# Expert weights and attention weights of the first half: the transfers start after ten gathers in place of two

## The chip, the core and the metric

One program on one core of a Trainium2 chip. The metric is the device time of one execution in microseconds (us). The five engines are called PE (matrix products), DVE (vector), ACT (scalar, activations), POOL (general) and SP (here it only issues transfers). Transfers issued by SP run on one hardware queue (q1), those issued by POOL on a software queue (q0); both are served by the core's 16 DMA engines.

## The reference

A block with three parts over x, 4 x 1024 tokens of width 256, all float32:

```python
x = x + 0.5 * ffn(layernorm(x), ...)      # mixture of 8 experts, first half
x = x + attn(layernorm(x), ...)           # gated recurrence, projections, MLP
x = x + 0.5 * ffn(layernorm(x), ...)      # the same 8 experts, second half

def ffn(tokens):                          # 4096 tokens
    probs = softmax(tokens @ gate_w + gate_b)
    expert_idx = argmax(probs)            # one expert for each token
    # the first 160 tokens of each expert are kept: 8 x 160 = 1280 slots
    h = gelu(dispatch @ w1[e] + b1[e])    # 256 -> 1024
    expert_out = h @ w2[e] + b2[e]        # 1024 -> 256
    # back to the token's row, times its probability; other rows get 0
```

The expert weights w1 and w2 have 1 MB each for each expert; the attention uses Wa (256 x 512), Wk, Wv, Wg, Wq, Wo (256 x 256), W1 (256 x 1024) and W2 (1024 x 256).

## The kernel before, in words

The program has three stages: the first expert half (about 0 to 142 us of the span), the attention (to about 620 us) and the second expert half. Only the first half is touched. Synchronisation is written by hand with semaphores: an engine's instructions run in the order of the code, and a wait holds back all that stands behind it on that engine.

**The first half on the computing engines.** x is read in 8 blocks (tiles `xc`), the gate's logits are computed, and a list of tokens for the 1280 slots is made. POOL then gathers the slots' rows from x in HBM with 10 indirect transfers of 128 rows each (L574, tile `xg`, semaphores `xg_in[0]` to `xg_in[9]`). DVE normalises a gathered tile (L240), PE turns it (L969, `turn_in`), ACT copies it to `xdt` (L811). An expert e is `up(e)` on PE (L982: 8 groups of products into four banks, each group followed by a GELU on ACT, L819) and `down(e)` (L995, then ACT L828). PE's order is turn_in 0 and 1, up(0), `list_gates` (L911), turn_in 2 to 4, up(1), turn_in 5 to 9, down(0), up(2), down(1), a turn_out (L1009), up(3), down(2), a turn_out, up(4), down(3) and so on to down(7). up(0) needs the gathers 0 and 1 alone, up(1) those up to 4 by the code's order. down(0) also waits for DVE's `idx_s` (L768), which stands behind all ten gathers' norms.

**The weights.** The experts' weights live in a ring of four buffers (`ring`, `GE = 4`): those of experts 0, 1 and 2 are fetched early, at 20 to 40 us; expert 3's (the "fourth expert's") goes to the fourth buffer, and those of 4 to 7 each to a buffer that a finished `down` sets free. `up(e)` waits for both transfers of expert e.

**The attention's raw weights.** DVE splits each weight matrix of the attention into a high and a low part (`w_in_h`, `w_in_l`, `w_h`, `w_l`; L776 and L778). There are ten pieces in this order: two of Wa, Wk, Wv, Wg, Wq (256 KB each), two of W1, two of W2 (512 KB each). They pass through the four `xc` buffers (`RB = 4`), so that piece n, from n = 4 on, is fetched only when piece n - 4 has been split (`raw_done`). DVE does the ten splits after `idx_s`, and only then the output tiles `xo` (L784).

**The copy.** The first half's result is x plus corrections in 1280 rows: one transfer copies all of x (4 MB) from HBM to `x_mid` in HBM (L528, semaphore `copied`), and POOL's indirect stores of the output tiles (L583) wait for it.

**SP's order** from expert 3 on is: wait for gathers, w1 and w2 of expert 3 (L513, L514), Wo (L520), pieces 0 to 3 (L524), the copy (L528), pieces 4 to 9 each after its `raw_done`, then w1 and w2 of expert 4, of 5, 6 and 7, each pair after a `down`. All of it runs on q1.

Of the kernel before, what the change touches and what calls it, by code (L numbers as in the profile page):

```python
# [28 lines left out]
ST = SLOTS // P  # L29
# [9 lines left out]
GT = GE * CAP // P  # L39
# [269 lines left out]
def expert_half(nc, turn, sems, src, dst, copy_from, norms, bank, cst, ring0, gate_w, gate_b, ew1, eb1, ew2, eb2,  # L309
# [5 lines left out]
    with ExitStack() as ctx:  # L315
# [4 lines left out]
        def sem(name):  # L320
            return sems.new(f"{name}_{turn}")
# [91 lines left out]
        xg_in = [sem(f"xg_in{a}") for a in range(ST)]  # L413
# [40 lines left out]
        def w1_of(s):  # L454
            return ring[s][:, 0:KD * F].rearrange("p (k f) -> p k f", k=KD)

        def w2_of(s):
            return ring[s][:, KD * F:WE].rearrange("p (m d) -> p m d", m=KF)
# [21 lines left out]
        def raw_view(n):  # L480

            shape = pieces[n][1].shape
            return xc[n % RB][:].rearrange("p a b -> p (a b)")[:, 0:shape[1] * shape[2]].rearrange(
                "p (k n) -> p k n", k=shape[1])

        def sync_program(sp):
            if first:

                ln1_s, ln1_b, b1 = norms
                for n in range(NB):  # L490
                    if n >= RB:
                        sp.wait_ge(tp_ready, KD * (n - RB + 1))
                        sp.wait_ge(var_ready, n - RB + 1)
                    sp.dma_start(xc[n % RB][:], src[n * BT:(n + 1) * BT, :].rearrange("(j p) d -> p j d", p=P)).then_inc(
                        x_in[n % RB], 16)
                    if n == 1:
                        sp.dma_start(cst["gate_w"][:], gate_w.rearrange("(k p) e -> p k e", p=P)).then_inc(gp_in, 16)
                        sp.dma_start(cst["gate_b"][:], gate_b.partition_broadcast(P)).then_inc(gp_in, 16)
                        sp.dma_start(cst["eb"][:], eb1.rearrange("e (m p) -> (e m) p", p=P)).then_inc(gp_in, 16)
                        sp.dma_start(cst["eb2r"][:], eb2.rearrange("e (m p) -> (e m) p", p=P)).then_inc(gp_in, 16)  # L500

            if first:
                for name, w in (("ln1s", ln1_s), ("ln1b", ln1_b), ("b1", b1)):
                    sp.dma_start(cst[name][:], w.rearrange("(k p) -> p k", p=P),
                                 allow_slow_non_contiguous=True).then_inc(ln1_in, 16)
            for e in range(NE):
                s = e % GE
                if e >= GE:
                    sp.wait_ge(down_ready, KD * (e - GE + 1))
                if first and e == GE - 1:  # L510
                    sp.wait_ge(xg_in[0], 16)
                    sp.wait_ge(xg_in[1], 16)
                sp.dma_start(w1_of(s), ew1[e].rearrange("(k p) f -> p k f", p=P)).then_inc(w_in[s], 16)  # L513
                sp.dma_start(w2_of(s), ew2[e].rearrange("(m p) d -> p m d", p=P)).then_inc(w_in[s], 16)  # L514
                if first and e == GE - 1:

                    sp.wait_ge(tp_ready, NB * KD)
                    sp.wait_ge(var_ready, NB)
                    wo = dense_src[5]
                    sp.dma_start(dense["wo_f"][:], wo.rearrange("(k p) n -> p k n", p=P)).then_inc(wo_in, 16)  # L520
                    for n, (piece, _, _) in enumerate(pieces):
                        if n >= RB:
                            sp.wait_ge(raw_done, n + 1 - RB)
                        sp.dma_start(raw_view(n), piece).then_inc(raw_in[n % RB], 16)  # L524
                        if n == RB - 1:
                            for a in range(GT):
                                sp.wait_ge(xg_in[a], 16)
                            sp.dma_start(dst, copy_from).then_inc(copied, 16)  # L528

        def gpsimd_program(pool):  # L530
# [305 lines left out]
        def tensor_program(pe):  # L836
# [176 lines left out]
            for name, n in expert_steps():  # L1013
                do[name](n)

        return Programs(sync_program, gpsimd_program, vector_program, scalar_program, tensor_program, scattered)


# [751 lines left out]
```

## Time and profile before

| | us |
|---|---|
| median of 3 runs | 725.93 (724.41 to 726.29) |
| the profiled execution | 726.66 |
| its span, first to last instruction | 725.0 |

The profile is one execution of its own, 0.73 us above the median. All times below are us from the start of its span. PE is busy for 89% of the span, DVE for 66%, ACT for 63%. In the rows, a number in square brackets is the idle time of the engine ahead of the instruction and what ended it; SPq is SP's transfer issue. "PEclk" is the granted share of PE's clock: 1.00 is 2.4 GHz, 0.50 is 1.2 GHz.

### The profile page before, as it was taken

The numbers are of one execution on the slowest core, as the hardware profiler recorded it, in microseconds if no ns is written. First come the engines' busy times: TensorE is split into PE (matmuls) and PEld (weight loads), VectorE is DVE, ScalarE is ACT, GpSimd is POOL, SyncE is SP. The second block draws the span as 40 slices with busy tenths as digits, with TensorE's granted clock in tenths as the row PEclk, the third lists the DMA queues.
The fourth block names the chain that finished last, engine by engine and source line by source line (L and its number), as shares of the span: only waits on it lengthen the run. The fifth ranks groups of instructions, "written<-read, shape, count | busy, mean of one in ns | idle before, by whom it ended". The sixth has DMA issues, their size and how long they took to land. (4 is left out here: it accounts for less than half of the span.)

```text
span 725.0 us, 11552 instructions
## 1 busy us (share of the span) xinstructions
PE 648.2 (89%) x4309; PEld 572.3 (79%) x4309; DVE 477.0 (66%) x1056; ACT 453.9 (63%) x815; POOL 196.6 (27%) x292
## 2 busy tenths in 40 slices
PE   8988999686879899999999899999997789799993
PEld 5457999555668889889899799898887689389993
DVE  5661700135697989989989989988989777520001
ACT  3314444037779889888898898898797243244440
POOL 6141011221013123424234234235125131420112
PEclk9997999899879999999999999999999799799997
DMA  6949882150101201202201220211011086117700
GB/s 206 330 161 381 285 289 80 50 166 31 57 29 59 73 1 46 73 1 74 74 19 56 73 69 7 72 44 41 4 44 44 1 296 227 52 37 238 248 23 24
DMA packets 48816, 74.07 MB, mean 102 GB/s; under 512 B 4614, under 2 KB 40539, under 8 KB 48696
## 3 DMA queue, kind: packets, MB, share of 16 engines
q1 hardware_dynamic: 44408, 59.84, 24.8%
q0 software_dynamic: 4352, 13.49, 5.2%
q8 instruction: 34, 0.56, 0.3%
q14 instruction: 22, 0.18, 0.1%
HBM read 62.45 MB, written 15.20 MB: 107 GB/s over the span
## 5 line engine op out<-in xcount | busy, mean ns | idle before, releaser
L1617 PE MATMUL bank<-zt_h,w_in_h 128*128 128x512 f32 x192 | 80.8, 421 | 14.5 <-DVE zt_l L1277 6.1
L982 PE MATMUL bank<-xdt,ring 128*128 128x160 f32 x512 | 78.8, 314 | 4.7 <-issue 3.6
L1617 PE MATMUL bank<-yt_h,w_h 128*128 128x256 f32 x256 | 74.4, 291 | 7.3 <-DVE yt_l L1402 6.3
L982 PEld LDWEIGHTS bank<-xdt,ring 128*128 128x128 f32 x512 | 75.4, 202 | 6.4 <-issue 6.0
L784 DVE SCALAR_TENSOR_TENSOR xo<-bank,gate,xg 128x256 f32<-128x256 f32 x20 | 9.3, 481 | 106.6 <-PE bank L1009 106.6
L1619 PE MATMUL bank<-zt_h,w_in_l 128*128 128x512 f32 x192 | 76.5, 399 | 0.0
L1618 PE MATMUL bank<-zt_l,w_in_h 128*128 128x512 f32 x192 | 76.4, 398 | 0.0
L1617 PE MATMUL bank<-w_h,ht_h 128*128 128x256 f32 x256 | 74.3, 290 | 0.0
L995 PE MATMUL bank<-hid,ring 128*128 128x160 f32 x512 | 72.8, 300 | 1.5 <-DVE idx_s L768 0.7
L1618 PE MATMUL bank<-w_l,ht_h 128*128 128x256 f32 x256 | 72.4, 283 | 0.0
L1619 PE MATMUL bank<-w_h,ht_l 128*128 128x256 f32 x256 | 72.3, 283 | 0.0
L995 PEld LDWEIGHTS bank<-hid,ring 128*128 128x128 f32 x512 | 70.4, 190 | 2.3 <-issue 2.3
L1618 PE MATMUL bank<-yt_l,w_h 128*128 128x256 f32 x256 | 72.2, 282 | 0.0
L1619 PE MATMUL bank<-yt_h,w_l 128*128 128x256 f32 x256 | 72.1, 282 | 0.0
L819 ACT ACTIVATE hid<-bank,b1t 128x160 f32<-128x160 f32 x128 | 50.1, 394 | 33.2 <-PE bank L982 8.4
L1150 POOL TENSOR_TENSOR rsq<-mvq,eps_ln 128x2 f32<-128x2 f32 x32 | 13.8, 432 | 207.9 <-DVE mvq L1253 207.9
L1593 ACT ACTIVATE hf<-bank,b_t 128x256 f32<-128x256 f32 x128 | 53.4, 469 | 18.5 <-PE bank L1619 13.6
L1617 PEld LDWEIGHTS bank<-yt_h,w_h 128*128 128x128 f32 x256 | 48.8, 191 | 10.5 <-DVE yt_l L1402 8.4
L1617 PEld LDWEIGHTS bank<-zt_h,w_in_h 128*128 128x128 f32 x192 | 37.2, 194 | 25.0 <-DVE qg L1292 7.8
L828 ACT ACTIVATE eot<-bank,b2t 128x160 f32<-128x160 f32 x32 | 12.6, 394 | 60.2 <-PE bank L995 60.2
L1618 PEld LDWEIGHTS bank<-yt_l,w_h 128*128 128x128 f32 x256 | 49.0, 191 | 0.7
L1618 PEld LDWEIGHTS bank<-w_l,ht_h 128*128 128x128 f32 x256 | 48.9, 191 | 0.4
(243 smaller groups left out, 1620.4 us busy)
## 6 DMA issues: line engine op xcount, KB each, us to landing
ring<-in_L_ffn_w SPq DMA_DIRECT2D x32, 1024.0 KB, 10.4
xc<-in_L_attn_x SPq DMA_DIRECT2D x8, 512.0 KB, 4.2
zb<-x_mid SPq DMA_DIRECT2D x8, 512.0 KB, 5.1
z_mid<-zb POOLq DMA_DIRECT2D x8, 512.0 KB, 3.4
zr<-z_mid SPq DMA_DIRECT2D x16, 256.0 KB, 2.9
xr<-x_mid SPq DMA_DIRECT2D x16, 256.0 KB, 3.6
out<-xq POOLq DMA_DIRECT2D x16, 256.0 KB, 4.2
xc<-in_L_attn_W SPq DMA_DIRECT2D x4, 512.0 KB, 5.3
```

Source lines behind the costliest of these rows:

```text
L784: V.scalar_tensor_tensor(xo[:, a % GT, :], bank[6 + a % 2][:, 0:D], gate[:, a:a + 1], xg[:, a, :], ALU.mult, ALU.add).then_inc(xo_ready, 1)
L819: S.activation(hid[:, e % 2, m, :], bank[b][:, 0:CAP], ACT.Gelu_apprx_tanh, bias=cst["b1t"][:, e * KF + m:e * KF + m + 1]).then_inc(gelu_d ...
L828: S.activation(eot[:, d, slots(e)], bank[4 + d][:, 0:CAP], ACT.Identity, bias=cst["b2t"][:, e * KD + d:e * KD + d + 1]).then_inc(eo_done, 1)
L982: ins = T.matmul(bank[b][:, 0:CAP], w1_of(s)[:, k, m * P:(m + 1) * P], xdt[:, k, e * CAP:(e + 1) * CAP], start=k == 0, stop=k == KD - 1)
L995: ins = T.matmul(bank[4 + d][:, 0:CAP], w2_of(e % GE)[:, m, d * P:(d + 1) * P], hid[:, e % 2, m, :], start=m == 0, stop=m == KF - 1)
L1150: own.step(G.tensor_tensor(rs[:], mv[:, :, 1], cst[eps][:, 0:n], ALU.add))
L1593: ins = S.activation(hf[m % 2][:, t, :], upb[m % 2][:, t * QW:(t + 1) * QW], ACT.Gelu_apprx_tanh, bias=b1_t[:, 2 * m + t:2 * m + t + 1])
L1617: T.matmul(out, left[0], right[0], start=start, stop=False)
L1618: T.matmul(out, left[0], right[1], start=False, stop=False)
L1619: return T.matmul(out, left[1], right[0], start=False, stop=stop)
```

## The change

SP waits for all ten gathers (ST = 10) in place of the first two ahead of expert 3's weights. The wait for five gathers ahead of the copy goes, since it is then always fulfilled. Nothing else differs: no transfer or instruction is added, removed or put in another order.

```diff
                 if first and e == GE - 1:
-                    sp.wait_ge(xg_in[0], 16)
-                    sp.wait_ge(xg_in[1], 16)
+                    for a in range(ST):
+                        sp.wait_ge(xg_in[a], 16)
                 sp.dma_start(w1_of(s), ew1[e].rearrange("(k p) f -> p k f", p=P)).then_inc(w_in[s], 16)
                 sp.dma_start(w2_of(s), ew2[e].rearrange("(m p) d -> p m d", p=P)).then_inc(w_in[s], 16)
...
                         if n == RB - 1:
-                            for a in range(GT):
-                                sp.wait_ge(xg_in[a], 16)
                             sp.dma_start(dst, copy_from).then_inc(copied, 16)
```

SP's program at expert 3's weights, as a difference (- before, + after; `ring_0` with the wait is expert 3's buffer, `xg_inN_0` the semaphore of gather N):

```order
 L513 DMA ring_0<-in_L_ffn_w 128x2x1024
 L514 DMA ring_0<-in_L_ffn_w 128x8x256
-L513 DMA ring_0<-in_L_ffn_w 128x2x1024 [waits xg_in1_0,xg_in0_0]
+L513 DMA ring_0<-in_L_ffn_w 128x2x1024 [waits xg_in5_0,xg_in6_0,xg_in4_0,xg_in7_0,xg_in3_0,xg_in8_0,xg_in2_0,xg_in9_0,xg_in1_0,xg_in0_0]
 L514 DMA ring_0<-in_L_ffn_w 128x8x256
 L520 DMA wo_f<-in_L_attn_Wo 128x2x256 [waits var_ready_0,tp_ready_0]
```

The place in the queue is the same; the wait ahead of it has eight more gathers in it.

SP's program at the copy, a few rows further on (`xc_0` are the raw pieces' buffers):

```order
 L524 DMA xc_0<-in_L_attn_Wk 128x2x256
 L524 DMA xc_0<-in_L_attn_Wv 128x2x256
-L528 DMA x_mid<-in_L_attn_x 64x16384 [waits xg_in3_0,xg_in2_0,xg_in4_0,xg_in1_0,xg_in0_0]
+L526 DMA x_mid<-in_L_attn_x 64x16384
 L524 DMA xc_0<-in_L_attn_Wg 128x2x256 [waits raw_done_0]
 L524 DMA xc_0<-in_L_attn_Wq 128x2x256 [waits raw_done_0]
```

The copy stays behind the four pieces and ahead of the other six, without a wait of its own.

## Rows read from the trace of the kernel before

**Rows 1.** Timeline of SP: start, length of the issue, line, transfer

```profile
48.50 0.37 SPq L513 DMA_DIRECT2D ring<-in_L_ffn_w  x1
...
53.08 0.80 SPq L524 DMA_DIRECT2D xc<-in_L_attn_Wv  x1
55.97 0.54 SPq L528 DMA_DIRECT2D x_mid<-in_L_attn_x  x1
73.86 0.38 SPq L524 DMA_DIRECT2D xc<-in_L_attn_Wg  x1
...
79.32 0.37 SPq L524 DMA_DIRECT2D xc<-in_L_attn_W  x1
79.73 0.51 SPq L513 DMA_DIRECT2D ring<-in_L_ffn_w  x1
86.19 0.37 SPq L513 DMA_DIRECT2D ring<-in_L_ffn_w  x1
86.60 0.47 SPq L514 DMA_DIRECT2D ring<-in_L_ffn_w  x1
...
95.52 0.47 SPq L514 DMA_DIRECT2D ring<-in_L_ffn_w  x1
```

**Rows 2.** Timeline of PE and ACT in up(0), first half

```profile
50.49 2.41 PE L982 MATMUL bank<-xdt,ring 128*128 128x160 f32 x16 [1.13 <-ACT xdt L811]
53.50 0.39 ACT L819 ACTIVATE hid<-bank,b1t 128x160 f32<-128x160 f32 x1 [3.15 <-remote]
53.94 0.81 PE L982 MATMUL bank<-xdt,ring 128*128 128x160 f32 x4 [1.04 <-issue]
```

**Rows 3.** Timeline of PE: down(0) and up(4), first half; up(0) and down(0), second

```profile
72.88 4.58 PE L995 MATMUL bank<-hid,ring 128*128 128x160 f32 x32 [0.37 <-DVE idx_s L768]
...
95.13 4.51 PE L982 MATMUL bank<-xdt,ring 128*128 128x160 f32 x32
...
632.83 6.95 PE L982 MATMUL bank<-xdt,ring 128*128 128x160 f32 x32 [0.56 <-issue]
...
649.87 4.58 PE L995 MATMUL bank<-hid,ring 128*128 128x160 f32 x32 [0.37 <-DVE idx_s L768]
```

**Rows 4.** Timeline of POOL: the last gather of either half

```profile
55.97 0.95 POOL L574 DMA_INDIRECT xg<-in_L_attn_x,idx_g  x1 [0.30 <-issue]
...
638.67 0.95 POOL L574 DMA_INDIRECT xg<-out,idx_g  x1 [0.31 <-issue]
```

**Rows 5.** Issues one by one: transfer, count, size, us from issue to landing

```profile
xc<-in_L_attn_Wv SPq DMA_DIRECT2D x1, 256.0 KB, 9.7
...
xg<-in_L_attn_x,idx_g POOLq DMA_INDIRECT x1, 5.9
x_mid<-in_L_attn_x SPq DMA_DIRECT2D x1, 18.4
...
xc<-in_L_attn_W SPq DMA_DIRECT2D x1, 512.0 KB, 5.9
...
ring<-in_L_ffn_w SPq DMA_DIRECT2D x1, 1024.0 KB, 8.9
...
ring<-in_L_ffn_w SPq DMA_DIRECT2D x1, 1024.0 KB, 11.0
...
ring<-in_L_ffn_w SPq DMA_DIRECT2D x1, 1024.0 KB, 8.2
...
xg<-out,idx_g POOLq DMA_INDIRECT x1, 3.1
```

**Rows 6.** Windows: stretch, us, busy PE, PEld, DVE, ACT, POOL, PEclk, DMA share, GB/s

```profile
50.00:54.00 4.00, 2.47 (x17) 2.26 (x17) 2.70 (x8) 0.74 (x2) 3.08 (x4) 1.00 0.94 361
...
74.00:78.00 4.00, 4.00 (x32) 4.00 (x31) 3.86 (x8) 0.79 (x2) 0.00 (x0) 1.00 0.56 179
...
90.00:94.00 4.00, 4.00 (x32) 4.00 (x31) 0.00 (x0) 1.26 (x4) 0.16 (x1) 1.00 1.06 386
...
570.00:573.00 3.00, 3.00 (x15) 2.91 (x14) 2.26 (x8) 0.00 (x0) 0.44 (x3) 0.53 0.01 3
```

**Rows 7.** Timeline of PE at its longest idle stretch in the attention

```profile
566.82 3.78 PE L1671 MATMUL bank<-wo_f,yo 128*128 128x256 f32 x8 [6.65 <-DVE yo L1381]
```

## The prediction

> **What bounds the kernel now.** I first read the timeline of PE over the first half, then set it beside the same code in the second half. In up(0), PE issues its first 16 product records within 2.41 us, but ACT gets the first GELU's input only at 53.50, after 3.15 us of idling, and PE, which needs that GELU for its next group, goes on at 53.94 [rows 2]. From the start of up(0) to the start of down(0) the first half takes 72.88 - 50.49 = 22.4 us, the second half, with the same instructions and the same ten gathers, 649.87 - 632.83 = 17.0 us [rows 2, 3]. The trace calls what ACT waited for "remote": it does not name what held PE's signal back. What differs between the halves is what else moves: the timeline of SP shows expert 3's weights, Wo and four raw pieces issued from 48.50 on [rows 1], and the windows show 361 GB/s in 50 to 54 [rows 6]. So the stretch may be 5.4 us shorter without them; and since PE's clock is granted in full there (1.00 [rows 6]) while up(0) of the second half runs 6.95 us against 4.51 for an expert at the full clock [rows 3], it may be 5.4 + 2.4 = 7.8 us shorter.
>
> From down(0) on PE runs without a gap of note, and up(4) starts at 95.13 [rows 3]. The second thing to read is therefore when expert 4's weights land. Their own landing has no row; that of their neighbours has. Expert 5's second transfer lands at 86.60 + 11.0 = 97.6, expert 6's at 95.52 + 8.2 = 103.7 [rows 1, 5]. One expert's 2 MB through the busy queue is 6.1 us, so expert 4 was in at about 97.6 - 6.1 = 91.5. That is 3.6 us ahead of need, and all of the first half's transfers stand ahead of it in one queue. The slack is small, and the change spends it.
>
> **The change, part by part.** *The added wait.* The last gather is issued at 55.97 and lands after 5.9 us now; in the second half, without other traffic, after 3.1 us [rows 4, 5]. With the traffic gone I take 3.1: SP goes on at 59.1 in place of 48.50, 10.6 us later. Behind the wait on SP stand w1 and w2 of expert 3, Wo, four pieces, the copy, six more pieces and the eight weights of experts 4 to 7. The *removed wait* ahead of the copy costs or saves nothing, since gathers 0 to 4 are in by then.
>
> *Up to the fourth piece.* Before, the transfers from expert 3's w1 (issued 48.50) to Wv (issued 53.08, landed 53.08 + 9.7 = 62.8) took 14.3 us [rows 1, 5]. The last seven gathers, issued 0.95 + 0.30 us apart [rows 4] and so from 48.5 on, shared that time: 7 x 128 KB are 0.92 MB, at 361 GB/s [rows 6] 2.5 us, which no longer fall in it. 59.1 + 14.3 - 2.5 = 70.9. Expert 3's weights, first in this stretch, are needed by up(3), which stands one expert (4.51 + 4.58, 9.1 us [rows 3]) ahead of up(4): at 86 before, at 78 at the soonest now. They are in time, so this part costs nothing. DVE's splits of the first four pieces began after idx_s, just ahead of 72.88; they begin at about 68 now, when the first piece lands, three pieces ahead of 70.9. PE waits for none of them.
>
> *The copy.* It landed at 55.97 + 18.4 = 74.4, 11.6 us after Wv [rows 1, 5]. Now: 70.9 + 11.6 = 82.5.
>
> *Behind the copy.* Before, DVE's splits asked for piece 4 only at 73.86, as the copy ended, so the copy held nobody back. Now DVE has split a piece by 70 and SP can issue the next, while the copy is still moving, and piece 4 has to stand behind it until 82.5. Pieces 4 to 9 are 2 x 256 + 4 x 512 KB = 2.6 MB, at 361 to 386 GB/s [rows 6] 6.8 to 7.3 us; I take 7.0. DVE's splits of pieces 4 and 5, after which SP may issue 8 and 9, fit into the time that pieces 6 and 7 take, so no bubble. Then expert 4: 6.1 us. 82.5 + 7.0 + 6.1 = 95.6.
>
> *The same from above.* From 48.50 to 91.5 the chain took 43.0 us. Less the gathers' 2.5, and less the time in which the queue waited for DVE: 74 to 78 moved 179 GB/s in place of 361, 2.0 us lost [rows 6]. 59.1 + 38.5 = 97.6. Between 95.6 and 97.6 I take the middle, 96.6; both ends stay in the range, with a microsecond more on each side for the copy. up(4) starts 96.6 - 95.1 = 1.5 us later than before.
>
> *The clock.* PE would be ready for up(4) 5.4 to 7.8 us earlier than before, at 87.3 to 89.7, and so it idles for 7 to 9 us. Of a wait of that length the attention has an example: PE idles 6.65 us until 566.82, and the windows show the clock at 0.53 of 2.4 GHz still in 570 to 573, that is half speed for 6 us after work began again [rows 6, 7]. Half speed costs half of that, 3.0 us. Bounds: nothing, if the clock isn't lowered, and 3 us or a little more. The idle time is as long as in that row, but there are shorter recoveries too, so I take 2.3.
>
> *The sum.* 1.5 + 2.3 = 3.8 us later at up(4). From there on PE is the bound to the end of the half: expert 5's weights land 6.1 us after expert 4's, and PE needs them 9.1 us after. The saved 5.4 to 7.8 us are worth nothing, since they end in a wait for expert 4. Nothing later absorbs the delay, because the attention starts after the last store. 726.66 + 3.8 = 730.5 for a profiled execution; the median of the runs is 0.73 lower, so 729.7.
>
> *A rule on the order.* Rows 5 show expert 5's first transfer landing at 95.1 and the second, issued 0.4 us later, at 97.6 [rows 1, 5]: the queue serves them one behind the other. No row shows a piece that was issued behind the running copy. The Trainium skill ("DMA: Bandwidth & Descriptors", section "Queues, rings and completion order") says that each DMA engine consumes a queue's descriptors in ring order; by that rule pieces 4 to 9 stand behind the whole copy, and the sum is the one above; if they could pass it, the time is that of the second rival.
>
> **The rivals.** *The slow up(0) stays.* Its cause isn't named in the trace, and could be the gathers or PE itself. For: gathers were in flight in the same microseconds. Against: the second half has them too and runs through. Then PE comes to up(4) at 95.1, waits 1.5 us, and the clock stays up: 728.2 profiled, 727.4 as a median, 726 to 729.5 with the chain's ends. Chance 0.15.
>
> *The copy holds nothing back, and the change is faster.* Place: pieces 4 to 9 and expert 4 behind the copy. If they get past or beside it, expert 4 lands up to 11.6 us sooner, at 85.0, PE never waits, and the whole 5.4 to 7.8 us is gained: 718.1 to 720.5. It decides as soon as expert 4 lands ahead of 89.7. For: no row shows such a queue. Against: the order seen for expert 5. Chance 0.12.
>
> *The queue is quicker than reckoned.* If it loses 2.5 to 4.5 us against my sum, for instance in the copy, expert 4 lands at 92 to 94; with 0 to 2.3 us of slow clock that is -3.1 to +1.2, so 722.8 to 727.1. Chance 0.13.
>
> **How the numbers follow.** The forecast, expert 4 late and PE idle ahead of it, has 0.60. Its own range is 727 (landing 95, 1.2 us of clock) to 733 (98.5, 3.7 us). A measurement tells 0.3%, 2.2 us, from no change: 723.7 to 728.1. Slower: 0.51 of the forecast and 0.05 of the first rival, 0.56. Faster: the 0.12 of the second rival and 0.04 of the third, 0.16. The rest, 0.28, is within 0.3%. The range 723 to 733.5 leaves out the second rival and a tail above.
>
> **What the changed profile would show.** SP's L513 for expert 3 at about 59; ACT's first GELU within 1.5 us of up(0)'s start, no "remote" there; down(0) at 65 to 67.5; the copy landing at 82 to 83; SP's issue of piece 4 at about 70 but its landing after the copy's; a PE gap of 7 to 9 us ahead of up(4), ended by `ring` and not by a GELU; PEclk at 0.50 in it and behind it; up(4) at 95.5 to 98. I'd be wrong if up(0) still took 9 us, if piece 4 landed well ahead of the copy, or if the clock stayed at 1.00 through the gap.

## The result and the profile after

| | before | changed |
|---|---|---|
| median of 6 runs each, side by side | 726.11 (724.41 to 728.19) | 733.53 (730.63 to 734.06) |
| the profiled execution | 726.66 | 733.6 |
| its span | 725.0 | 731.9 |

The changed kernel is slower: the ratio is 1.0086, with a 95% interval of 1.0065 to 1.0107. The prediction had the sign; its 729.7 is 3.8 us short: it forecast 3.8 us more than its median of before, and side by side 7.4 us are measured. The median stands 0.03 us above the upper end of its range of 723 to 733.5.

The timeline of SP in the changed kernel, to be read beside [rows 1] (start, length of the issue, line, transfer; two lines of the code have gone, so L526 is the copy):

```profile
58.01 0.37 SPq L513 DMA_DIRECT2D ring<-in_L_ffn_w  x1
...
61.57 1.47 SPq L524 DMA_DIRECT2D xc<-in_L_attn_Wv  x1
63.08 1.08 SPq L526 DMA_DIRECT2D x_mid<-in_L_attn_x  x1
69.02 0.38 SPq L524 DMA_DIRECT2D xc<-in_L_attn_Wg  x1
...
71.14 14.64 SPq L524 DMA_DIRECT2D xc<-in_L_attn_W  x4
85.83 0.51 SPq L513 DMA_DIRECT2D ring<-in_L_ffn_w  x1
86.38 0.47 SPq L514 DMA_DIRECT2D ring<-in_L_ffn_w  x1
```

The same issues one by one, beside [rows 5], with the us from issue to landing in the last column (POOL's first gather, then in the order of SP's timeline Wv, copy, Wg, expert 4's w1):

```profile
xg<-in_L_attn_x,idx_g POOLq DMA_INDIRECT x1, 3.6
...
xc<-in_L_attn_Wv SPq DMA_DIRECT2D x1, 256.0 KB, 8.3
x_mid<-in_L_attn_x SPq DMA_DIRECT2D x1, 19.5
...
xc<-in_L_attn_Wg SPq DMA_DIRECT2D x1, 256.0 KB, 14.1
...
ring<-in_L_ffn_w SPq DMA_DIRECT2D x1, 1024.0 KB, 8.1
```

The stream begins at 58.0, 9.5 us later than before. Wv lands at 61.57 + 8.3 = 69.9, the copy at 63.08 + 19.5 = 82.6. The row to learn from is Wg: 256 KB, issued at 69.0 while the copy was moving, lands after 14.1 us at 83.1, just behind the copy. Before, Wg took 2.7 us, since it was only asked for at 73.86, half a microsecond before the copy landed. The trace agrees here with the ring order that the prediction weighed. It does not show that the order in the ring is the reason: in e3 below, gathers on another queue wait for the copy too.

Next the timeline of PE in the changed kernel, from up(0) to down(3), and its start in the attention (in brackets the idle time and what ended it). These rows answer to [rows 2] and [rows 3]:

```profile
48.94 4.58 PE L980 MATMUL bank<-xdt,ring 128*128 128x160 f32 x32 [0.56 <-ACT xdt L809]
...
63.75 4.58 PE L993 MATMUL bank<-hid,ring 128*128 128x160 f32 x32 [0.37 <-DVE idx_s L766]
...
85.78 0.38 PE L1007 MATMUL bank<-ident,eot 128*128 128x128 f32 x2
97.00 7.06 PE L980 MATMUL bank<-xdt,ring 128*128 128x160 f32 x32 [10.84 <-DMA ring<-in_L_ffn_w]
103.90 4.37 PE L993 MATMUL bank<-hid,ring 128*128 128x160 f32 x31
...
148.09 11.56 PE L1622 MATMUL bank<-iota_p,ones_h 128*128 128x512 bf16 x41 [6.19 <-POOL rsz L1144]
```

up(0) now runs through in 4.58 us. PE is ready for up(4) at 86.2, waits 10.84 us for expert 4's weights, and then up(4) takes 7.06 us in place of 4.51. The windows of the changed kernel say why, beside [rows 6] (stretch, us, busy PE, PEld, DVE, ACT, POOL, PEclk, DMA share, GB/s):

```profile
84.00:88.00 4.00, 2.16 (x17) 1.92 (x15) 3.88 (x7) 0.60 (x2) 0.00 (x0) 1.00 0.71 234
88.00:102.00 14.00, 5.00 (x19) 5.00 (x20) 5.76 (x7) 1.50 (x4) 2.03 (x2) 0.51 1.03 362
...
163.50:167.00 3.50, 3.50 (x10) 2.69 (x9) 0.62 (x6) 0.60 (x1) 1.57 (x4) 0.52 0.33 115
```

From 88 to 102 the granted clock is 0.51 of 2.4 GHz, the 1.2 GHz level: it fell during the wait and came back only after up(4) had run at half speed for some 5 us. The DMA engines were full over this stretch as a whole (1.03, 362 GB/s): the queue was busy with work that came late. Just before it, from 84 to 88, they were not (0.71, 234 GB/s). The first piece behind the copy landed at 83.1, DVE had to split it, and only then, at 84.36, did SP ask for piece 8, and at 85.42 for piece 9; expert 4 stands behind both. That is some 1.9 us of the queue's time (an estimate: 235 GB/s over the 5 us from 84 to 89, against 377 from 92 to 96).

The account from before to after: up(4) starts 97.00 - 95.13 = 1.9 us later; it takes 7.06 - 4.51 = 2.6 us longer; up to the last store nothing more is lost (144.26 against 139.84, 4.4); PE's wait ahead of the attention's first product is 0.4 us longer (6.19 against 5.80; 148.09 against 143.28 for its end, 4.8 in all). From there to the span's end it is 731.9 - 148.1 = 583.8 us against 725.0 - 143.3 = 581.7, another 2.1 us in a part of the program that the change does not touch. One place of it is the last window above. In the attention products of the same shape stand 0.23 us apart before and 0.42 us apart in the changed kernel, here two neighbours in either timeline of PE (first before, with the window around them, then changed):

```profile
158.00:162.00 4.00, 4.00 (x19) 3.31 (x18) 0.39 (x6) 2.01 (x4) 1.58 (x4) 1.00 0.36 123
...
159.16 0.39 PE L1618 MATMUL bank<-zt_l,w_in_h 128*128 128x512 f32 x1
159.39 0.39 PE L1619 MATMUL bank<-zt_h,w_in_l 128*128 128x512 f32 x1
```

```profile
163.99 0.63 PE L1617 MATMUL bank<-zt_h,w_in_l 128*128 128x512 f32 x1
164.41 0.63 PE L1615 MATMUL bank<-zt_h,w_in_h 128*128 128x512 f32 x1
```

The first twelve of these products take 4.45 us in the changed kernel (162.49 to 166.94) and 2.86 before (156.75 to 159.61), so 1.6 us are lost in this stretch at the lower clock, which the profile of before does not have there.

The change can't be named as the cause of the 2.1 us. From the attention's first product on, the fourteen profiles of this document fall into two kinds. In three (before, e2 and g1, which is the kernel before again) the clock is back 2.4 to 2.9 us behind that product, no lowered stretch follows 14 to 20 us behind it, and this part of the program takes 581.1 to 581.7 us. In the other eleven it is back after 3.9 to 6 us, there is such a stretch, and the part takes 583.5 to 586.3 us. Among the eleven are the kernels below in which expert 4 is never late (e3, f1 to f4, g3, g4).

### The profile page after: what moved, and what is told of

It reads as the page before. It is cut to its first block and busy times, and to the rows that moved or that the text cites. A ratio compares the mean times of both kernels' runs of the same rounds, so it can differ in the third digit from the quotient of the medians.

```text
span 731.9 us, 11550 instructions
## 1 busy us (share of the span) xinstructions
PE 646.5 (88%) x4305; PEld 572.3 (78%) x4309; DVE 476.9 (65%) x1056; ACT 454.0 (62%) x815; POOL 195.8 (27%) x292
## 5 line engine op out<-in xcount | busy, mean ns | idle before, releaser
L1615 PE MATMUL bank<-zt_h,w_in_h 128*128 128x512 f32 x192 | 81.3, 423 | 14.1 <-DVE zt_l L1275 6.1
L980 PE MATMUL bank<-xdt,ring 128*128 128x160 f32 x512 | 77.4, 312 | 12.0 <-DMA ring<-in_L_ffn_w 10.8
L1616 PEld LDWEIGHTS bank<-yt_l,w_h 128*128 128x128 f32 x256 | 48.9, 191 | 0.7
L1669 PE MATMUL bank<-wo_f,yo 128*128 128x256 f32 x128 | 34.7, 418 | 16.6 <-DVE yo L1379 16.6
```

What stands on the lines that cost most here:

```text
L980: ins = T.matmul(bank[b][:, 0:CAP], w1_of(s)[:, k, m * P:(m + 1) * P], xdt[:, k, e * CAP:(e + 1) * CAP], start=k == 0, stop=k == KD - 1)
L1615: T.matmul(out, left[0], right[0], start=start, stop=False)
L1616: T.matmul(out, left[0], right[1], start=False, stop=False)
L1669: ins = T.matmul(o_attn[:, t * D:(t + 1) * D], yo[:, k, c], wo_f[:, k, :], start=k == 0, stop=k == KD - 1)
```

## The experiments

Two things in this looked open. One is whether the delay really comes out of the queue behind the copy, and how it divides between landing and clock. The other is why up(0) was slow before. Each kernel is one edit of the changed kernel unless said otherwise. The experiments ran on three chips, called A, B and C here; each ratio is to the kernel before on the same chip.

### The delay: e1 to e4 (chip A, before at 726.6)

**e1_five** waits for five gathers in place of ten.

```diff
-                    for a in range(ST):
+                    for a in range(GT):
                         sp.wait_ge(xg_in[a], 16)
```

> The changed kernel, with SP waiting for five gathers ahead of the fourth expert's weights in place of ten. My theory (all transfers stand in one queue, and expert 4's weights come at its end): gathers 0 to 4 are in at 51.2 us in the changed kernel's trace, 6.7 us ahead of the tenth, and gathers 5 to 9 take back some 1.8 us of the queue's time, so expert 4's weights land about 4.9 us earlier, at 92; PE still waits about 6 us for them, with the slow clock behind the wait; the half ends where it ended before the change, 725 to 729 us. Rival (gathers and queue traffic together slow up(0), whatever the number): the stream starts at about 53, as up(0) ends, but then meets up(1); if that is slowed, down(0) starts at 66 or later instead of 63.8, and the time is the same all the same, since the wait for expert 4 absorbs it.

Measured: 729.59 (729.15 to 731.29), ratio 1.0038 [1.0025, 1.0051]. Timelines of SP and PE of this kernel:

```profile
51.69 0.37 SPq L513 DMA_DIRECT2D ring<-in_L_ffn_w  x1
...
92.97 7.54 PE L980 MATMUL bank<-xdt,ring 128*128 128x160 f32 x32 [6.37 <-DMA ring<-in_L_ffn_w]
```

The stream begins 6.3 us sooner than with ten gathers, up(4) starts 4.0 us sooner, and the median is 3.9 us lower (not measured side by side). The wait's length reaches the end of the program through expert 4's landing. The median is 0.6 us above the 725 to 729 expected. The clock's part does not shrink with the gap: after 6.4 us of idling up(4) takes 7.54 us, after 10.8 it took 7.06.

**e2_copy_last** issues the copy behind expert 7's weights; nothing in the queue stands behind it then.

```diff
                         sp.dma_start(raw_view(n), piece).then_inc(raw_in[n % RB], 16)
-                        if n == RB - 1:
-                            sp.dma_start(dst, copy_from).then_inc(copied, 16)
+            if first:
+                sp.dma_start(dst, copy_from).then_inc(copied, 16)
```

> The changed kernel, with the 4 MB copy of x to x_mid issued behind the weights of expert 7. My theory (the running copy holds back pieces 4 to 9 and expert 4): piece 4 lands at 72 or earlier in place of 83, expert 4's weights land at about 84 to 86, the 10.8 us gap of PE ahead of up(4) goes, and with it the slow clock; up(4) starts at about 86. The copy then ends at 107 to 114 and holds back the stores, which may cost 0 to 4 us at the sixth output tile: 717 to 723 us. Rival (the ten gathers' wait alone makes expert 4 late, the copy doesn't matter): expert 4 lands at 94 or later, PE's gap stays, 731 us or more.

Measured: 719.24 (717.16 to 722.42), ratio 0.99 [0.9871, 0.9928]. Its timelines of SP and PE, and behind them its issue of Wg by itself, with the us to landing:

```profile
68.08 0.37 SPq L524 DMA_DIRECT2D xc<-in_L_attn_Wg  x1
...
85.62 4.61 PE L981 MATMUL bank<-xdt,ring 128*128 128x160 f32 x32 [0.50 <-DMA ring<-in_L_ffn_w]
...
133.87 10.66 PE L1623 MATMUL bank<-iota_p,ones_h 128*128 128x512 bf16 x42 [5.80 <-POOL rsz L1145]
```

```profile
xc<-in_L_attn_Wg SPq DMA_DIRECT2D x1, 256.0 KB, 2.8
```

With all ten gathers waited for as in the changed kernel, and only the copy out of the way, Wg lands after 2.8 us in place of 14.1, up(4) starts at 85.6 in place of 97.0, its clock stays up (4.61 us), and the attention starts at 133.9 in place of 148.1. This settles the mechanism of the delay: the late start of the stream becomes a late expert 4 only because the copy stands between them. The same pair of kernels was run side by side on chip C below (g2 and g3): there too the gap goes, and the time falls by 8.0 us.

**e3_copy_first** issues the copy behind expert 2's weights, ahead of the wait for the gathers.

```diff
                 if first and e == GE - 1:
+                    sp.dma_start(dst, copy_from).then_inc(copied, 16)
                     for a in range(ST):
                         sp.wait_ge(xg_in[a], 16)
```

> The changed kernel, with the copy issued behind expert 2's weights, ahead of the wait for the ten gathers. My theory: the queue is empty from 40 us on, the copy uses that time and ends at 51 to 53; expert 4's weights land at 83 to 86, no gap ahead of up(4). The copy now shares the DMA engines with the gathers: the first two may land up to 2 us later. Expected 717 to 722 us. Rival A (any traffic beside the gathers slows up(0)): up(0) takes 6 to 9 us again, as before the change, down(0) starts at 67 to 71, still no gap ahead of up(4), 720 to 725 us. Rival B (only transfers that write into the core's memory beside the gathers slow up(0)): up(0) takes 4.6 us.

Measured: 725.88 (723.42 to 728.41), ratio 0.9983 [0.9965, 1.0001]. Expert 4 is no longer late: up(4) starts at 93.13 without a gap. But the time went elsewhere. The timelines of SP (the copy), POOL (the first gather) and PE, and behind them the same two issues with their us to landing:

```profile
28.42 4.60 SPq L511 DMA_DIRECT2D x_mid<-in_L_attn_x  x1
...
42.60 1.80 POOL L571 DMA_INDIRECT xg<-in_L_attn_x,idx_g  x1 [18.39 <-DVE idx_g L674]
...
52.85 1.16 PE L966 MATMUL bank<-ident,xn 128*128 128x128 f32 x4 [5.41 <-DVE xn L240]
...
54.58 6.10 PE L979 MATMUL bank<-xdt,ring 128*128 128x160 f32 x32 [0.56 <-ACT xdt L808]
```

```profile
x_mid<-in_L_attn_x SPq DMA_DIRECT2D x1, 23.6
...
xg<-in_L_attn_x,idx_g POOLq DMA_INDIRECT x1, 9.7
```

The copy, issued at 28.42, lands at 52.0. The first gather, issued at 42.6 on the other queue, lands at 52.3, after 9.7 us in place of 3.6 in the changed kernel. The gathers issued behind it, at 44.7 to 49.7, land 0.3 to 0.4 us after one another from 52.6 to 54.0. So the copy is in the way of the gathers too, and PE turns the first tile 5.6 us late. It only has another place in which to hurt.

**e4_busy** keeps PE busy ahead of up(4) with 45 products that nobody reads.

```diff
+                if first and e == GE:
+                    pe.wait_ge(gelu_done[0], 2 * e)
+                    for _ in range(45):
+                        T.matmul(bank[0][:], cst["ones_h"][:],
+                                 cst["iota_p"][:, 0:BT // CT, :].rearrange("p a b -> p (a b)"),
+                                 start=True, stop=True)
```

> The changed kernel, with 45 products without use (128 columns by 512, bf16, into a free bank) on PE ahead of the wait for expert 4's weights, some 10.4 us of work in a gap of 10.8. My theory (half of what up(4) and its neighbour lose is the clock that falls in the gap): PEclk stays at 1.00 from 57 to 140, up(4) takes 4.5 us in place of 7.1, and the time falls by 2.5 us or a little more to 730 to 731.5 us; expert 4's weights land at 97 as before. Rival (the whole loss is the late landing): no difference, 733.5 us.

Measured: 730.82 (728.21 to 732.52), ratio 1.0046 [1.0026, 1.0066]. Its timeline of PE, and behind it its window:

```profile
87.34 9.88 PE L976 MATMUL bank<-iota_p,ones_h 128*128 128x512 bf16 x45
...
146.16 11.76 PE L1628 MATMUL bank<-iota_p,ones_h 128*128 128x512 bf16 x42 [5.79 <-POOL rsz L1150]
```

```profile
88.00:102.00 14.00, 13.30 (x73) 8.09 (x72) 6.73 (x9) 2.37 (x6) 2.03 (x2) 1.00 1.02 362
```

The clock stays at 1.00 where it was 0.51. up(4) starts at 97.9, 0.9 us later than in the changed kernel, and still the attention starts 1.9 us sooner. Of these 2.8 us up(4) itself gives 2.45 (4.61 in place of 7.06 us), and that is the clock's part. The other 0.4 is PE's wait ahead of the attention, 5.79 us here and 6.19 in the changed kernel; it is 5.8 in all four profiles of chip A and 6.2 in all eight of chips B and C, so nothing ties it to the clock. Between the medians it is 2.7 us (733.53 and 730.82), but they were not measured side by side, and the two ratios' intervals just touch; the trace carries this reading, not the medians.

### The slow up(0): f1 to f4 (chip B, before at 726.91)

The prediction took expert 3's stream beside the gathers as the cause of the slow up(0), and in the traces of after and e1 to e4 none was as slow as before's (e3's 6.10 us goes with late gathers and a lowered clock). The four kernels all have the copy last, so that expert 4 is not late and up(0) shows in the time. They put different parts of the stream beside the gathers (shortened; lines with + and - are the code's):

```diff
 f1_two_copy_last: the kernel before, with the copy behind expert 7's weights
 f2_weights_early: as f1, and behind w2 of expert 3
+                    for a in range(ST):
+                        sp.wait_ge(xg_in[a], 16)
 f3_pieces_early: as f1, but Wo and pieces 0 to 3 ahead of
+                    for a in range(ST):
+                        sp.wait_ge(xg_in[a], 16)
                 sp.dma_start(w1_of(s), ...)
 f4_five_copy_last: as e2_copy_last, with
-                    for a in range(ST):
+                    for a in range(GT):
```

> The kernel before the change (wait for two gathers), with the copy issued behind expert 7's weights. It is the fourth corner of the change and the place of the copy. My theory (the early stream beside the gathers is what slows up(0), and the copy has no part in that): up(0) takes 8 to 10 us from its start to list_gates again, with signals of PE reaching ACT late; down(0) starts at about 72 to 73, PE reaches up(4) at 94 to 95, expert 4 is in by then, the half ends within 1 us of where it did before: 724 to 727 us. Rival (the slow up(0) of the trace before was the copy's or the profile's, or chance): up(0) takes 4.6 us, down(0) starts at 64 to 66, and the time is that of the changed kernel with the copy last, 717 to 721 us.

> Copy last, and only expert 3's two weight transfers (2 MB) issued after two gathers; Wo and the raw pieces wait for all ten. If any stream beside the gathers slows up(0): up(0) takes 6 us or more, down(0) at 68 to 72, 721 to 726 us. If it takes the whole stream or the SP queue being busy with many issues: up(0) takes under 5.5 us, 717 to 721 us.

> Copy last, and only Wo and the first four raw pieces (1.25 MB, 3.5 us of the queue) issued after two gathers; expert 3's weights wait for all ten. If any stream beside the gathers slows up(0), it does so for 3.5 us at most: up(0) takes 5 to 8 us, down(0) at 65 to 69, 719 to 723 us. If only the large weight transfers into the ring do it: up(0) takes 4.6 us and the time is 717 to 720 us.

> Wait for five gathers and the copy last. My theory (with the copy out of the way the queue is early enough either way, and the stream after five gathers comes too late to meet up(0)): the same as ten gathers with the copy last, 717 to 721 us, with expert 4's weights in at 79 to 82 rather than 85.6 and no wait at all ahead of up(4), 0 to 1 us less. Rival (gathers 5 to 9 beside the stream slow up(1)): down(0) starts 1 us or more later, 720 to 722 us.

| | median | ratio | down(0) starts | up(4) starts |
|---|---|---|---|---|
| f1_two_copy_last | 727.22 | 1.0002 [0.9973, 1.003] | 69.06 | 91.31 |
| f2_weights_early | 727.75 | 1.0008 [0.9979, 1.0037] | 69.74 | 91.99 |
| f3_pieces_early | 729.47 | 1.0023 [1.0001, 1.0045] | 69.83 | 92.08 |
| f4_five_copy_last | 727.63 | 0.9991 [0.9969, 1.0014] | 68.00 | 90.25 |

All four medians lie above what was expected, f3 and f4 by 6 us and more. These four did not tell the parts of the stream apart: whatever is beside the gathers, down(0) starts at 68.0 to 69.8, where e2 on chip A has 62.7. f4 is the telling one. Its timeline, with PE, ACT and SP:

```profile
51.08 2.41 PE L981 MATMUL bank<-xdt,ring 128*128 128x160 f32 x16 [0.68 <-ACT xdt L810]
...
52.62 0.37 SPq L513 DMA_DIRECT2D ring<-in_L_ffn_w  x1
...
53.87 0.39 ACT L818 ACTIVATE hid<-bank,b1t 128x160 f32<-128x160 f32 x1 [2.94 <-remote]
```

In e1_five the first GELU starts 0.82 us behind up(0) (50.20 behind 49.38). Here it would be due at 51.9, and it comes at 53.87, although SP has issued nothing since expert 2's weights until 52.62. The program is e1_five's up to the copy, and the copy is not issued until the late signals are past; e1_five's down(0) starts at 64.19, f4's at 68.00. The transfers can't be what makes the difference.

The copy's late place has a price of its own here. The first store waits for it, until 120.4 to 123.3 in the six profiles of f1 to f4, g3 and g4 and 86.9 in g1, and from up(4) to the attention they take 48.9 to 50.0 us against 48.6 in g1.

The late signals don't always stand at the same step. In f1, f4, g2 and g3 they are ACT's "remote" waits inside up(0), in f2, f3, g1 and g4 PE idles 3.3 us ahead of it and its clock falls. Of the latter g1_before below has this row in its timeline of PE, and this window:

```profile
52.49 7.19 PE L982 MATMUL bank<-xdt,ring 128*128 128x160 f32 x32 [3.30 <-ACT xdt L811]
```

```profile
55.00:59.00 4.00, 4.00 (x21) 4.00 (x21) 0.00 (x0) 1.95 (x5) 1.45 (x2) 0.65 1.08 344
```

### The same on a third chip: g1 to g4 (chip C, before at 727.39)

The last four had to tell whether the slow up(0) belongs to the program or to the chip. g1_before is the kernel before, g2_after the changed kernel, g3_ten_last is e2_copy_last and g4_five_last is f4_five_copy_last, each letter for letter.

> The kernel before the change, unchanged, profiled on the same chip as the three that follow. So far the slow up(0) stands in the trace before the change and in the four traces of one chip, and in none of the five traces of kernels on other chips, of which one (wait for five, copy in its old place) is the same program as one of the slow ones up to 56 us. Theory K (the kernel's stream beside the gathers slows up(0)): up(0) takes 9 to 10 us here (7 to 8 with its start late) and the ten-gather kernels take 4.6. Theory C (it belongs to the chip or the execution, not to the place of the stream): all four kernels of this call show it, or none does. If none: down(0) here starts at 64 to 66 and PE waits for expert 4's weights, up(4) at 90 to 93. 724 to 729 us either way.

> The changed kernel, unchanged, on the same chip. Theory K: up(0) in 4.6 us, down(0) at 64, a PE gap of 9 to 11 us ahead of up(4) at 97; 731 to 734 us. Theory C on a slow chip: up(0) slow too, down(0) at 67 to 70, the gap ahead of up(4) 4 to 6 us; still 730 to 734 us, since expert 4's landing sets the time.

> Ten gathers and the copy behind expert 7's weights, again. Theory K: 717 to 722 us as on the first chip, 4 us or more below g4. Theory C: on a chip with fast signals 717 to 722 us, on one with slow ones 722 to 728 us, in both cases within 3 us of g4_five_last.

> Five gathers and the copy last, again (727.6 us on a chip on which the trace showed slow signals). Theory K (the stream beside gathers 5 to 9 is what makes the difference to g3): 724 to 729 us and up(0) slow, while g3 is at 717 to 722. Theory C: within 3 us of g3_ten_last, and up(0) slow in both or in neither.

| | median | ratio | down(0) starts | up(4) starts |
|---|---|---|---|---|
| g1_before | 726.43 | 1.0004 [0.9975, 1.0034] | 69.90 | 92.15 |
| g2_after | 735.71 | 1.0138 [1.0099, 1.0177] | 71.38 | 99.53 |
| g3_ten_last | 727.67 | 1.0001 [0.9976, 1.0026] | 69.44 | 91.69 |
| g4_five_last | 729.63 | 1.0045 [1.0016, 1.0074] | 69.95 | 92.19 |

The timeline of g2_after, the changed kernel on this chip, with PE, ACT and SP:

```profile
50.95 2.96 PE L980 MATMUL bank<-xdt,ring 128*128 128x160 f32 x20 [1.17 <-ACT xdt L809]
...
54.73 0.39 ACT L817 ACTIVATE hid<-bank,b1t 128x160 f32<-128x160 f32 x1 [2.45 <-remote]
...
55.18 0.81 PE L980 MATMUL bank<-xdt,ring 128*128 128x160 f32 x4 [1.28 <-ACT hid L817]
56.16 0.39 ACT L817 ACTIVATE hid<-bank,b1t 128x160 f32<-128x160 f32 x1 [1.04 <-remote]
...
59.38 0.37 SPq L513 DMA_DIRECT2D ring<-in_L_ffn_w  x1
...
99.53 6.63 PE L980 MATMUL bank<-xdt,ring 128*128 128x160 f32 x32 [5.74 <-DMA ring<-in_L_ffn_w]
```

Here SP issues nothing from expert 2's weights until 59.38, and up(0) has the same stops, each behind a "remote" wait of ACT, as in [rows 2]. Its down(0) starts at 71.38, 7.6 us later than in the first profile of the very same kernel (63.75). All four kernels show the slow up(0), and g3 and g4 lie 2.0 us apart, as expected if it does not hang on the stream. The theory that it takes expert 3's stream to make up(0) slow has fallen. The delay itself stands: side by side with the kernel before, the changed kernel is slower by 1.4% here, and with the copy last (g3) it is as fast as before. And on this chip e2's copy-last order, which took 7 us off the kernel before's time on chip A, is worth nothing against it: PE reaches up(4) at 91.7 by itself, and expert 4 had no part in that.

## Why the prediction was right, point by point

**The stream starts at 59.1.** It started at 58.0. The last gather was issued a microsecond sooner than before and landed after 3.0 us (3.1 taken from [rows 4, 5]); only its start was off.

**Wv at 70.9, the copy at 82.5.** They landed at 69.9 and 82.6. The copy took 12.7 us behind Wv in place of 11.6, which made up for Wv's early landing.

**Pieces 4 to 9 behind the copy, expert 4 at 96.6.** The order is right: e2 took the copy away, and the whole delay went. Expert 4's w1, issued at 85.83, landed at 93.9; its w2, issued at 86.38, landed after 10.6 us, at 97.0, where up(4) starts. The size is in part luck. From the copy to expert 4 the forecast had 7.0 + 6.1 = 13.1 us, and it took 97.0 - 82.6 = 14.4. The step that was wrong is "so no bubble": DVE could not split pieces 4 and 5 ahead of time, because they had only just landed, and the queue ran at 234 GB/s from 84 to 88. A start of the stream 1.1 us too late in the forecast, and the middle taken between 95.6 and 97.6, made up for it.

**up(4) 1.5 us later, the clock 2.3.** They are 1.9 and 2.6, and e4 confirms the second by taking 2.45 of it away. The gap was 10.8 us and not 7 to 9, because PE was ready at 86.2 and not at 87.3 to 89.7; as the forecast had it, that costs nothing, since the end of the gap is set by the queue.

**"Nothing later absorbs the delay."** True, but something later added to it, and the sum has no term for it: 0.4 us in the wait ahead of the attention and 2.1 us behind it. Those 2.5 us are most of what separates the 733.6 profiled from the 730.5 forecast for it. The rest of the program takes 581.6 us behind e2's first half (715.5 less 133.9), 581.7 behind before's, 584.4 behind e4's (730.6 less 146.2) and 583.8 behind the changed one's. Over all fourteen profiles it takes 581.1 to 586.3, with no order by how late expert 4 was: this untouched part varies by up to 5 us from one profile to another. That the stretch at the lower clock at 163 to 167 is part of it is shown; what puts it there is not, and so the 2.1 us can't be counted as the change's.

**The slow up(0).** The step "the stretch may be 5.4 us shorter without them" named a cause that isn't needed. f1 to f4 and g1 to g4 show the slow up(0) whatever SP moves, and with nothing of SP's in flight in g2 and g3. It did not spoil the time, because the forecast priced these microseconds at zero. It does decide how the change looks: where up(0) runs through, PE idles 10.8 us ahead of up(4), where it does not, 5.7 us. In both cases up(4) starts when expert 4 has landed, so the first rival (up(0) stays slow, 1.5 us of wait and no clock cost, 727.4) had its premise come true on chip C, and its price not: expert 4 was in only at 99.5 there, PE idled 5.74 us, up(4) took 6.63 us at a lowered clock, and the time was 735.71.

**The other rivals.** That the copy holds nothing back fell with Wg's 14.1 us. That the queue is quicker than reckoned fell too: expert 4 landed 0.4 us later than its sum had it, not 2.5 to 4.5 sooner.

**What stays open.** Why PE's signals reach ACT late in up(0) in some profiled executions (before's, all eight of chips B and C) and not in others (the first of the changed kernel, all four of chip A). It lies in the microseconds in which POOL issues the gathers, but POOL does so in all of them. That the chip decides it fits the twelve profiles of the experiments, each chip having all of one kind, but no kernel was profiled twice on one chip, and the kernel before was not profiled on chip A. Nor is it on record which chips the first two profiles come from; if it was one chip, the chip does not decide it, since before's is of one kind and the changed kernel's of the other. The traces with the late signals also lack records: in all nine of them the first nine of the ten gathers of the first half have no landing (in f3, g2 and g3 all ten), and in the five others each has one. So the recording itself may have a part. The Trainium skill ("Perfetto Trace Analysis", section "Tensor Engine Instruction (MATMUL, LD_WEIGHTS)") says that a product's end in the profile is an estimate, and that its signal goes out only when PSUM has acknowledged the writes; by that, a part of the gap between the end of PE's rows and ACT's start can lie on the product's way out. No run here says which part of that path was slow. Whether e2's order beats the kernel before is open as well: 0.99 on chip A, 1.0001 on chip C. On neither was it measurably slower. An estimate, not a measurement, for chip A: if up(0) runs through there before the change as well, expert 4's landing near 91.5 is already too late for a PE that is ready near 86, and e2 gains what the kernel before loses by that.

## What to carry to other kernels

When a wait is added ahead of a transfer, go down its queue to the next thing that the bounding engine needs, and add up every transfer on the way: here the slack was 3.6 us by the prediction's estimate and the shift 9.5, and a 4 MB copy that nobody needed for 31 us (issued at 63.1, the first store at 94.6) stood in between. Look also at what comes between: here six pieces now had to pass behind the copy, and two of them could be asked for only when others had landed and been split. With the stream late, the long copy belonged behind everything that was needed soon (e2's attention starts 14.2 us sooner than the changed kernel's, and on chip C the same edit takes 8.0 us off its time); with the stream early it made no measurable difference (f1). Looking for it in only one queue is not enough, as e3 shows. And read a small difference against a trace of the kernel before from the same chip: the changed kernel alone reached down(0) at 63.8 us in one profile and at 71.4 in another.

## What was not expected of the hardware

A copy from HBM to HBM on one queue held back gathers on another: 9.7 us for the first one in place of 3.6, and it landed 0.3 us after the copy. The Trainium skill ("DMA: Bandwidth & Descriptors", section "Queues, rings and completion order") says that each DMA engine goes round between the queues in turn, packet by packet; by that I had expected the gathers to get their share. The trace of e3 shows little of it: not one of the gathers issued from 42.6 on landed before 52.3.

Between gaps of 5.7 and 10.8 us the clock's price did not grow with the gap: against 4.51 us, up(4) lost 2.6 us after 10.8 us of idling, 3.0 after 6.4 (e1) and 2.1 after 5.7 (g2). It lost 0.1 after 0.5 (e2), and as little when PE was kept busy (e4).

The kernel before varied from 721.12 to 729.73 us over 34 of its 35 runs on chip B (one more took 732.38) and from 722.79 to 730.0 over 29 on chip C, 1.2% and 1.0%, more than most differences sought here; the intervals of the ratios carry this.
